# A mixture-of-experts kernel on one core: 24 of the last stage's 96 gathers moved into the expert stage, that stage written anew

## What is computed

```python
x = x + attention(gate(x, fs, cond), Wq, Wk, Wv, Wo)         # 16 heads
g = gate2(x, fs, cond).reshape(2048, 512)
scores  = sigmoid(g @ gate_w)                                # 32 experts, 4 groups, best 2 groups are masked out
experts = top_k(masked scores, 6); weights = scores of these / their sum
d = silu(g @ w_gate[e]) * (g @ w_up[e]) @ w_down[e]          # for each token and each of its 6 experts, width 352
shared  = silu(g @ sw_gate) * (g @ sw_up) @ sw_down          # width 704
out = x + sum over the 6 experts of weight * d + shared
```

## Time and profile before

| | us |
|---|---|
| three runs, median (lowest, highest) | 2470.41 (2468.43, 2471.7) |
| the profiled execution, its own time | 2471.61 |
| its span, first to last instruction | 2469.9 |
| experts, from the first store of a block to the last | 1428.3 to 2313.0 |
| combining | 2315.8 to 2469.9 |

### The profile page before, as it was taken

The page is one execution under the profiler, slowest core; times in us unless marked ns, Lnnn a source line. Parts: engine busy times, 40 slices in busy tenths (PEclk is TensorE's granted clock), DMA queues, the critical chain, the costliest instruction groups (busy, mean ns, idle before and its releaser), DMA issues. The chain is left out here.

```text
span 2469.9 us, 42008 instructions
## 1 busy us (share of the span) xinstructions
PE 2253.3 (91%) x12059; PEld 1931.8 (78%) x12060; DVE 1266.8 (51%) x2118; ACT 1165.3 (47%) x2503; POOL 1444.7 (58%) x980
## 2 busy tenths in 40 slices
PE   2899999999999999898989899999999799999776
PEld 1678888888888877776778699999988699999654
DVE  8767777777766656758643322222222122222365
ACT  4467777777777767776621123333332133333210
POOL 7877777777755558566713144441579956430376
PEclk9999999999999999999979999999999899999988
DMA  4533444443354456453357144442557655442476
GB/s 116 162 95 111 123 129 158 149 129 120 119 184 143 132 179 200 142 172 108 130 204 283 46 138 158 137 156 88 170 171 228 195 170 182 149 168 76 122 206 183
DMA packets 285670, 372.37 MB, mean 151 GB/s; under 512 B 20212, under 2 KB 187192, under 8 KB 280824
## 3 DMA queue, kind: packets, MB, share of 16 engines
q1 hardware_dynamic: 231224, 252.46, 32.7%
q10 hardware_dynamic: 38976, 68.17, 8.4%
q0 software_dynamic: 15360, 50.34, 6.2%
HBM read 257.66 MB, written 113.25 MB: 150 GB/s over the span
## 5 line engine op out<-in xcount | busy, mean ns | idle before, releaser
L1925 POOL TENSOR_SCALAR we_high<-we_raw 128x1408 fp32r<-128x1408 f32 (+1 forms) x95 | 134.0, 1410 | 396.5 <-PE up_e L650 315.9
L1927 POOL TENSOR_TENSOR we_low<-we_raw,we_high 128x1408 fp32r<-128x1408 f32 (+1 forms) x95 | 314.5, 3311 | 7.9
L2056 DVE TENSOR_TENSOR hT_low<-hT_ps,hT_high 128x256 fp32r<-128x256 f32 x127 | 54.0, 425 | 391.5 <-ACT hT_high L2019 391.5
L2069 DVE TENSOR_TENSOR hidden_e<-silu_e,up_e 128x352 f32<-128x352 f32 x127 | 66.2, 521 | 283.5 <-ACT silu_e L2030 283.5
L2030 ACT ACTIVATE silu_e<-gate_e 128x352 f32<-128x352 f32 x127 | 59.0, 465 | 316.7 <-PE up_e L650 316.7
L650 PE MATMUL gate_e<-we_high,xT_high 128*128 x508 | 177.7, 350 | 20.8 <-POOL we_low L1927 20.4
L2035 ACT ACTIVATE rows_out<-down_e 128x512 f32<-128x512 f32 x127 | 75.9, 598 | 215.5 <-PE down_e L650 215.5
L650 PE MATMUL gate_e<-we_high,xT_low 128*128 x508 | 166.0, 327 | 0.0
L650 PE MATMUL gate_e<-we_low,xT_high 128*128 x508 | 165.7, 326 | 0.0
L650 PE MATMUL up_e<-we_high,xT_high 128*128 x508 | 164.4, 324 | 0.0
L650 PE MATMUL up_e<-we_low,xT_high 128*128 x508 | 163.1, 321 | 0.0
(11 more groups left out here) (341 smaller groups left out, 7341.8 us busy)
## 6 DMA issues: line engine op xcount, KB each, us to landing
rows_early<-slots_in ACTq DMA_DIRECT2D x129, 256.0 KB, 2.7
slots_out<-rows_out ACTq DMA_DIRECT2D x127, 256.0 KB, 2.0
we_raw<-L_ffn_w_gate SPq DMA_DIRECT2D x32, 704.0 KB, 4.4
we_raw<-L_ffn_w_up SPq DMA_DIRECT2D x32, 704.0 KB, 5.0
w_ring<-L_attn_Wq SPq DMA_DIRECT2D x64, 256.0 KB, 3.2
q_T<-q_out SPq DMA_DIRECT2D x64, 256.0 KB, 2.5
w_ring<-L_attn_Wk SPq DMA_DIRECT2D x64, 256.0 KB, 3.5
w_ring<-L_attn_Wv SPq DMA_DIRECT2D x64, 256.0 KB, 3.9
```

The lines of the kernel that those rows point to most:

```text
L1925: nc.gpsimd.tensor_scalar(wh[:, p, at:to], raw[:, at:to], 1.0, 1.0, ALU.mult, ALU.mult).then_inc(w_hi, 1)
L1927: nc.gpsimd.tensor_tensor(wl[:, p, at:to], raw[:, at:to], wh[:, p, at:to].bitcast(F32), ALU.subtract).then_inc(w_split, 1)
L2069: nc.vector.tensor_tensor(hb[:], sg[:], psu[:], ALU.mult).then_inc(h_done, 1)
```

## The change

- 24 row sets, of the first four tiles, are gathered in the expert stage. POOL does it behind the split of `sw_down`, once the count of evictions shows that all real blocks are stored (the number comes from `blocks`), with two gathers in flight on two semaphores. They go to places that are free by then (`row_homes`): the raw weights (8), the batch of x1 (4), the ends of the first halves of `we_high` and `we_low` (2 each), and a new tile for 8. The other 16 places are the second halves of the weight buffers.
- In the combining stage POOL issues the other 72, one after the other, each straight from `yslot` with no copy. Each waits for the landing of the gather four before it, on four semaphores. A place is used again when the tile that read it is done.
- DVE reads the weights in place. Its order is: low parts of tiles 0 and 1, then for each tile n the sum and the low part of n+2.
- PE reads x1 in place and has four PSUM banks. `xT` holds two batches: those of the first two are loaded in the expert stage, the third behind tile 3, the fourth behind tile 7.
- The loops of the stage are written out.
- Since gathers and stores of empty blocks now overlap, the places of `ys` that no real block is sure to fill (31 blocks) are zeroed: in the first stage SP writes one block of zeros to memory, and in attention steps 8 to 15 ACT's queue copies it to four blocks each (three in the last).

The removed lines of `combine` are the ones printed above and are left out here.

```diff
@@ -32,6 +32,7 @@
...
+NREAL = T * TOPK // P
...
@@ -125,7 +126,7 @@
...
-        qo = two("q0_out")
+        qo, zero = two("q0_out"), sb("zero_rows0", [P, C])
...
@@ -165,6 +166,8 @@
...
+            sp.wait_ge(ident_steps, 3)
+            sp.dma_start(dr["zeros"], zero[:]).then_inc(keep["spare_out"], 16)
...
@@ -192,6 +195,7 @@
...
+            sp.wait_ge(keep["spare_out"], 16)
...
@@ -199,6 +203,9 @@
...
+            pool.wait_ge(ident_steps, 2)
+            nc.gpsimd.memset(zero[:], 0.0).then_inc(ident_steps, 1)
+            pool.wait_ge(ident_steps, 3)
...
@@ -445,6 +452,9 @@
...
+SPARE = -(-(NBLK - NREAL) // (NIT - NFIRST))
...
@@ -1294,10 +1304,18 @@
...
+            def zero_blocks(j):
+                first = NREAL + SPARE * j
+                n = min(SPARE, NBLK - first)
+                act.dma_start(dr["ys"][first * P:(first + n) * P, :].rearrange("(n p) c -> p n c", p=P),
+                              dr["zeros"].unsqueeze(1).broadcast_to([P, n, C])).then_inc(keep["spare_out"], 16)
...
+                if it >= NFIRST:
+                    zero_blocks(it - NFIRST)
...
@@ -1353,6 +1371,7 @@
...
+            act.wait_ge(keep["spare_out"], 16 * (NIT - NFIRST + 1))
...
@@ -1836,6 +1855,9 @@
...
+MORE = 8
+IN_FLIGHT = 4
+EARLY_ROWS = 16 + MORE
...
@@ -1844,10 +1866,18 @@
...
+def row_homes(keep):
+    flat = lambda t: (t if t.dtype == F32 else t.bitcast(F32))[:, 0:t.shape[1] // C * C].rearrange("p (k c) -> p k c", c=C)
+    homes = (flat(keep["we_raw"][:]), keep["x1"][:], flat(keep["we_high"][:, 0, SD_N:]), flat(keep["we_low"][:, 0, SD_N:]),
+             keep["more_rows"][:], flat(keep["we_high"][:, 1, :]), flat(keep["we_low"][:, 1, :]))
+    return [home[:, k, :] for home in homes for k in range(home.shape[1])]
...
+    ident, tab, blocks, yslot, xT = (keep[k] for k in ("ident", "tab", "blocks", "yslot", "xT"))
...
@@ -1868,8 +1898,8 @@
...
+        d_mm, y_ev, pool_steps, x1_in = sem("down_mm"), sem("rows_left_e"), keep["pool_steps"], keep["x1_in"]
+        sd_in, early_in = sem("sd_loaded"), [sem("early_rows_in0"), sem("early_rows_in1")]
...
@@ -1894,10 +1924,10 @@
...
+            for b in range(2):
...
+            sp.wait_ge(x1_in, 32)
...
@@ -1932,6 +1962,7 @@
...
@@ -1947,6 +1978,18 @@
...
+            real = pool.value_load(blocks[0:1, E - 1:E], min_val=NREAL, max_val=NBLK)
+            pool.wait_ge(y_ev, real + (CREDIT + 2))
+            pool.sem_inc(pool_steps, 1)
+            homes = row_homes(keep)
+            for i in range(EARLY_ROWS):
+                t, k = divmod(i, TOPK)
+                if i >= 2:
+                    pool.wait_ge(early_in[i % 2], 16 * (i // 2))
+                pool.indirect_dma_start(homes[i], None, dr["ys"],
+                                        bass.IndirectOffsetOnAxis(ap=yslot[:, t, k:k + 1], axis=0)).then_inc(early_in[i % 2], 16)
+            for q in range(2):
+                pool.wait_ge(early_in[q], 16 * EARLY_ROWS // 2)
...
@@ -2039,6 +2082,7 @@
...
+                act.sem_inc(y_ev, 1)
...
@@ -2074,126 +2118,106 @@
...
+    xT, ident, hsh, wts, yslot = (keep[k] for k in ("xT", "ident", "hsh", "wts", "yslot"))
...
+    tail = SCH[-1][1]
...
+        acc = sb("acc", [P, 2, C])
+        ob = keep["early"][:, 0:2, :]
+        homes = row_homes(keep)
+        row_of = lambda i: homes[i % len(homes)]
+        landed = lambda q, i: sum(j % IN_FLIGHT == q for j in range(EARLY_ROWS, i))
+        pso = [ctx.enter_context(nc.psum_tensor(f"out_ps{i}", [P, S], F32)) for i in range(4)]
+        hi, lo, y_in, acc_done = sem("h_hi6"), sem("h_lo6"), [sem(f"y_in{q}") for q in range(IN_FLIGHT)], sem("acc_steps")
+        o_mm, o_done, o_out = sem("out_mm"), sem("out_done"), [sem("out0"), sem("out1")]
...
+        at = lambda n: slice(P * n, P * n + P)
...
+            for n in range(NT):
+                b, t = divmod(n, TC)
+                if t == 0 and 0 < b < B - 1:
+                    sp.wait_ge(o_mm, n)
+                    sp.dma_start(xT[:, (b + 1) % 2, :, :], dr["x1"][b + 1].rearrange("p (k s) -> p k s", k=KC)).then_inc(keep["x1_in"], 16)
+                sp.wait_ge(o_done, n + 1)
+                sp.dma_start(out[b, at(t), :], ob[:, n % 2, :]).then_inc(o_out[n % 2], 16)
...
+                sp.wait_ge(o_out[p], 16 * NT // 2)
...
+            for i in range(EARLY_ROWS, NT * TOPK):
+                n, k = divmod(i, TOPK)
+                turn = i % IN_FLIGHT
+                if landed(turn, i):
+                    pool.wait_ge(y_in[turn], 16 * landed(turn, i))
+                if i >= len(homes) and (i == len(homes) or not (i - len(homes)) % TOPK):
+                    pool.wait_ge(o_done, (i - len(homes)) // TOPK + 1)
+                pool.indirect_dma_start(row_of(i), None, dr["ys"],
+                                        bass.IndirectOffsetOnAxis(ap=yslot[:, n, k:k + 1], axis=0)).then_inc(y_in[turn], 16)
...
+            for n in range(NT):
+                p, bank = n % 2, pso[n % 4]
+                parts = [((hh[0:w, p, c, :], hl[0:w, p, c, :]), (wh[0:w, c, :], wl[0:w, c, :])) for c, (_, w) in enumerate(SCH)]
+                pe.wait_ge(lo, n + 1)
+                if n >= 4:
+                    pe.wait_ge(o_done, n - 3)
+                split_products(nc, bank[:], parts[:1], True, False)
+                b, t = divmod(n, TC)
+                if t == 0 and b >= 2:
+                    pe.wait_ge(keep["x1_in"], 16 * (b + 1))
...
+                    nc.tensor.matmul(bank[:, k * P:(k + 1) * P], xT[:, b % 2, k, t * P:(t + 1) * P], ident[:], start=False, stop=False)
+                split_products(nc, bank[:], parts[1:], False, True).then_inc(o_mm, 1)
...
+            def high(n):
+                if n >= 2:
+                    act.wait_ge(o_mm, n - 1)
+                nc.scalar.activation(hh[:, n % 2, 0:NS - 1, :], hsh[:, 0:NS - 1, at(n)], ACT.Copy)
+                nc.scalar.activation(hh[0:tail, n % 2, NS - 1, :], hsh[0:tail, NS - 1, at(n)], ACT.Copy).then_inc(hi, 1)
+            for n in range(NT):
+                high(n)
...
+            tt = nc.vector.tensor_tensor
+            def low(n):
+                p = n % 2
+                dve.wait_ge(hi, n + 1)
+                tt(hl[:, p, 0:NS - 1, :], hsh[:, 0:NS - 1, at(n)], hh[:, p, 0:NS - 1, :].bitcast(F32), ALU.subtract)
+                tt(hl[0:tail, p, NS - 1, :], hsh[0:tail, NS - 1, at(n)], hh[0:tail, p, NS - 1, :].bitcast(F32),
+                   ALU.subtract).then_inc(lo, 1)
+            low(0)
+            low(1)
+            for n in range(NT):
+                p = n % 2
+                dve.wait_ge(o_mm, n + 1)
+                if n >= 2:
+                    dve.wait_ge(o_out[p], 16 * (n // 2))
+                for k in range(TOPK):
+                    last = k == TOPK - 1
+                    if TOPK * n + k >= EARLY_ROWS and (k == 0 or TOPK * n + k == EARLY_ROWS):
+                        for q in range(IN_FLIGHT):
+                            dve.wait_ge(y_in[q], 16 * landed(q, TOPK * (n + 1)))
+                    if k:
+                        dve.wait_ge(acc_done, (TOPK - 1) * n + k)
+                    nc.vector.scalar_tensor_tensor(out=(ob if last else acc)[:, p, :], in0=row_of(TOPK * n + k), scalar=wts[:, n, k:k + 1],
+                                                   in1=acc[:, p, :] if k else pso[n % 4][:], op0=ALU.mult,
+                                                   op1=ALU.add).then_inc(o_done if last else acc_done, 1)
+                if n + 2 < NT:
+                    low(n + 2)
...
@@ -2210,6 +2234,7 @@
...
+        zeros=dram("zero_block", [P, C]),
...
@@ -2220,7 +2245,6 @@
...
-            act_steps=top.enter_context(nc.semaphore("act_steps")),
...
@@ -2237,7 +2261,7 @@
...
-        for n in ("u_hi", "u_lo", "q_mm", "q_left", "q_out", "xt_out"):
+        for n in ("u_hi", "u_lo", "q_mm", "q_left", "q_out", "xt_out", "spare_out"):
...
@@ -2257,6 +2281,7 @@
...
+                keep["x1_in"] = moe.enter_context(nc.semaphore("x1_loaded_e"))
...
@@ -2265,8 +2290,8 @@
...
-                keep["xT"] = s3("xT", [P, B, KC, S])
...
+                keep["xT"], keep["more_rows"] = s3("xT", [P, 2, KC, S]), s3("expert_rows_more", [P, MORE, C])
...

```

More of the change, by code:

```diff
@@ L2083, in combine @@
         hh, hl = sb("h_high", [P, 2, NS, P], F32R), sb("h_low", [P, 2, NS, P], F32R)
[L2084 to L2087, removed]
-        acc, ob = (keep["early"][:, 2 * i:2 * i + 2, :] for i in range(2))
-        pso = [ctx.enter_context(nc.psum_tensor(f"out_ps{i}", [P, S], F32)) for i in range(2)]
@@ L2090, in combine @@
-        hi, lo, x_c, o_mm = sem("h_hi6"), sem("h_lo6"), sem("x1_copied"), sem("out_mm")
-        idx_done, y_in, acc_done, o_done, o_out = (sem("slot6"), [sem("y_in0"), sem("y_in1")], sem("acc_steps"), sem("out_done"),
-                                                   [sem("out0"), sem("out1")])
-        pool_steps, act_steps = keep["pool_steps"], keep["act_steps"]
-        block = ctx.enter_context(nc.Block())
-        tail = SCH[-1][1]
-        def loop(eng, step):
```

(49 more changed lines are left out.)

45 lines of the change are left out of this document (removed).

## The result

The changed kernel takes 2440.5 us (median of four runs, 2439.1 to 2444.85) where the kernel before took 2469.52 beside it: a ratio of 0.9884, interval 0.9867 to 0.9902. The forecast was 2437, in a range from 2419 to 2458. In a second series the ratio was 0.9895 (0.9878 to 0.9911). The profiled execution has a span of 2437.8 us.

The account below looks back on a forecast made before the run. POOL's gathers and the gaps between them were taken to bound the last stage. Gathers to the last store gave a span of 2432.3, plus 2 for x1 and 1.5 for zeros, 2435.8 us; forecast 2437, range 2419 to 2458.

Parts of the forecast that it names:

- A: Combining stage: POOL's gathers set the end, slowed by a busy DVE; forecast 2437 us, 2430 to 2448; chance 0.60.
- Early gathers, hidden: Expert stage: 24 gathers from about 2233, 2.0 us each, done at about 2281; 34 us of cover left, no cost.
- Start of the stage: Combining stage: first gather at 2316.2, about 0.7 us sooner; DVE starts at 2325.5.
- DVE sets the pace up to step 9: Combining stage: DVE steps of 5.6 us without a gap to 2381.5, from there DVE waits for gathers.
- Length of the run of gathers: Combining stage: gathers 1.26 us apart at first, 1.57 beside a busy DVE, the last 28 at 1.38; last start 2420.1.
- Four in flight seldom stop anything: Combining stage: landings of 3.4 to 5.1 us seldom hold a gather behind the fourth before it; nothing taken.
- Part 4: Combining stage: two x1 loads of 1 MB take DMA time from gathers; 2 us, bounds 0 to 7.
- rival C: Combining stage: the four in flight bind from a landing of 6.3 us on; with 7 us, time 2458; chance 0.13.
- Zeros: Last 8 attention steps: DRAM-to-DRAM zero copies on ACT's queue cost 1.5 us, between nothing and 29.
- Behind the last gather: End of combining: landing 4.4 us, six multiply-adds 4.7, store 3.0 after the last gather's start.
- Rival B: Combining stage: gathers aren't slowed and stay 1.26 us apart, DVE is the bound; time 2421; chance 0.15.
- D: Combining stage: gathers gated on the fourth before, slower than before from landings of 8.0 us; at 8.3, 2481; chance 0.04.

Follow-up runs that it names:

- best: Changed kernel with sum in PSUM, six in flight, x1 by tiles and zeros written behind the fills of the last routing stage: 2420.71 us, 0.9787 of the kernel before.
- in_flight_6: Changed kernel with six gathers in flight in the last stage instead of four: 0.9852 of the kernel before.
- sum_in_psum: Changed kernel with each tile's running sum kept in PSUM instead of SBUF: 0.9839 of the kernel before.
- zeros_later: Changed kernel with zeros written by SP's queue out of SBUF behind the last routing stage's fills, not by ACT's in the attention: 0.9859 of the kernel before.

## Why the prediction was right

The mechanism was A: POOL's gathers set the end, slowed by DVE. That 2437 comes so near 2440.5 is in part luck, since errors of several us cancelled. By its own steps:

- **Early gathers, hidden.** Right, in both their place and their pace: 2.08 us apart against 2.0. The gate opened at 2224, not 2233. Four evictions behind the last of expert 30 are enough (2223.00 is the fourth), so the last expert has two blocks and not the four that I took. The cover was 46 us instead of 34.
- **Start of the stage.** The first gather is 3.3 us behind the 2316.2 of the sum, and DVE's first sum at 2328.44 is 8.9 us behind it, against 9.3.
- **DVE sets the pace up to step 9.** The first wait does stand before tile 9, but this is luck. It came from 1.57 us for every gather from the eighth on, as long as DVE is busy. With six in flight or without the x1 loads DVE waits for no gather before tile 12. What brought the wait forward to tile 9 is the time that POOL stood still behind the two x1 loads, which the sum didn't have.
- **Length of the run of gathers.** 103.9 us and 2 for x1 in the sum, 106.8 measured. But here two terms were off and cancelled. Without the waits the run is 100 us: I had taken 1.57 us for every gather beside a busy DVE, and only 34 of 72 are slow, since a gather that starts inside the first multiply-add of a tile, or between two instructions, isn't held up. The waits are 6.8 us and I had 2.
- **Four in flight seldom stop anything** (part 3). This step failed. It took the landing times from a stage without loads of 1 MB. Part 4 put such a load only as DMA time shared out evenly, 3.6 us for 1 MB against 0.3 of free engines. What counts is that for some us no gather lands (4.7 us from 2352.1 on and 5.0 from 2374.4 on), and that a gate on the fourth before turns that into idle time of the bound engine. This is rival C's mechanism, in two short spells. Part 4's bounds of 0 to 7 held its cost. The runs with six in flight, without the loads and with small loads show it from three sides. That a satisfied wait costs nothing was right: the gap between two gathers is 0.30 us with it, as it was without.
- **Zeros.** 1.5 us in the sum, 3.7 measured alone (1.2 to 6.2 by the interval), against an upper bound of 29.
- **Behind the last gather.** 12.1 us from the last gather to the end in the sum, 2437.8 - 2426.27 = 11.5 measured.

Rival B was wrong for this kernel, yet it is what best comes to: 2420.71 us against the 2421 of B. The rule of the Trainium skill that I had set against the rows, SBUF — State Buffer, practical consequences, has two halves. That a DVE instruction with two SBUF inputs contends with GpSimd's reads over a read interface that they share, and one with a single SBUF input doesn't, agrees with the runs: with one of the inputs in PSUM 7 gathers are slow, with both in SBUF 34. The inference beside it, that such instructions leave descriptor generation alone, doesn't carry over to these gathers: they went from 0.95 to 1.27 us and more. A gather also reads its slot numbers out of SBUF (`yslot`), and whether that reading or the descriptors are held up isn't separated by any run. I had cited the rule only against the rows; its first half names the cure.

The mechanism of C and D is real: with two in flight the kernel is slower than before, and with four it cost 7 us. Landings went beyond D's 8.0 us (8.7), but only for a few gathers, and D needed it for all.

Open is why the time of in_flight_6, sum_in_psum and zeros_later fell by a few us more than their share in the trace. The intervals allow for it.

## What to carry to other kernels

Before a gate of "n in flight" is called free, look for what else will be in the queues at that time: a burst of 1 MB took landings from 5 to 8.7 us, and the engine whose issue sets the pace stood still; cutting the burst or opening the gate by two cost nothing. When one engine's instruction gets longer beside another's, look at where the other's operands lie before taking work away; moving the running sum to PSUM gave as much as leaving out four of six multiply-adds. Work moved under a stage with an idle engine is free only up to its side effects: here the zeros that the move needed cost a tenth of its gain.

## What I had not expected of the hardware

- A gather of 128 rows of 2 KB is issued in 0.95 us with 0.30 us between two. In `best` this pace nearly holds (1.28 us) at a DMA share of 0.88, from 2320 to 2400. A gather that starts while a DVE instruction with two inputs in SBUF is running ends 0.82 us behind that instruction's end, so that many take 1.22 to 1.37 us.
- A multiply-add of 128x512 f32 that reads and writes its sum in PSUM takes 0.78 us, as long as one in SBUF.
- Loads of 1 MB on another queue delay gathers that are already issued: landings up to 8.7 us instead of 5.5. With pieces of 256 KB it is 6.1.
- 7.75 MB of copies from memory to memory in the attention, where PE is busy over 90% of the time, cost 3.7 us, and nothing that could be seen where they went out of SBUF in the stage behind it.
